# A fused decoder layer: the mLSTM's value products move 65 columns instead of 128

## What is computed

```
qk = einsum('bhsd,bhtd->bhst', qh, kh) / sqrt(64)
C  = qk * D                                   # D: causal decay weights from the gates
normalizer = maximum(abs(sum(C, axis=-1)), exp(-max_log_D))
h  = einsum('bhst,bhtd->bhsd', C / (normalizer + EPS), vh)
h  = (h - mean(h)) * rsqrt(var(h) + 1e-5) * outnorm_scale     # per head
```

## Time and profile before

| | |
|---|---|
| median of 3 runs | 722.97 us (722.48 to 723.44) |
| span of the profiled execution, first to last instruction | 720.5 us |
| its own time outside the span | not listed apart; the median of the runs is 2.5 us over the span |
| TensorE (PE) busy | 622.3 us, 86% |
| weight loads (PEld) busy, beside PE | 451.7 us, 63% |
| VectorE (DVE) busy | 602.0 us, 84% |
| ScalarE (ACT) busy | 566.9 us, 79% |
| GpSimd (POOL) busy | 505.9 us, 70% |
| granted TensorE clock, mean | 0.955 of full speed |
| period of one sequence in the middle of the run | 37.6 us |

### The profile page before, as it was taken

One profiled execution on the slowest core, in us unless ns is written; L12 is line 12 of the kernel. 1 busy time (PEld: TensorE's weight loads), 2 busy tenths in 40 slices (PEclk: granted clock), 3 DMA queues, 4 the chain that ended last, 5 costly groups with the idle time before them and its releaser, 6 DMA issues. The chain is left out here.

```text
span 720.5 us, 16641 instructions
## 1 busy us (share of the span) xinstructions
PE 622.3 (86%) x4892; PEld 451.7 (63%) x4892; DVE 602.0 (84%) x2387; ACT 566.9 (79%) x1189; POOL 505.9 (70%) x781
## 2 busy tenths in 40 slices
PE   5688998999999999999999999998988978684642
PEld 3465785777767676867686868676665746452311
DVE  2475798999999999999999999998979998685853
ACT  1165979899998989898989898988769687875531
POOL 3185678778897878888888888875968746644432
PEclk9599999999999999999999999999999999898856
DMA  8995939455556575647273737454194611111201
GB/s 237 142 214 119 131 76 137 98 89 123 85 104 103 104 105 101 106 93 114 78 113 83 115 66 132 70 100 79 57 131 82 115 42 46 21 61 37 73 16 44
DMA packets 106104, 69.20 MB, mean 96 GB/s; under 512 B 47200, under 2 KB 106016, under 8 KB 106016
## 3 DMA queue, kind: packets, MB, share of 16 engines
q1 hardware_dynamic: 106016, 68.14, 51.9%
HBM read 28.73 MB, written 4.26 MB: 46 GB/s over the span
## 5 line engine op out<-in xcount | busy, mean ns | idle before, releaser
L2774 DVE CUSTOM_DVE_ANT_0 sc<-pS,bias 128x256 f32<-128x256 f32 x512 | 198.5, 415 | 25.6 <-PE pS L291 18.4
L1444 POOL TENSOR_SCALAR sc<-sc,mx 128x256 f32<-128x256 f32 x336 | 166.5, 506 | 28.1 <-DVE mx L2774 27.0
L1895 ACT ACTIVATE pr<-pT 128x512 f32<-128x512 f32 x256 | 152.2, 614 | 16.4 <-PE pT L309 16.1
L309 PE MATMUL pT<-ident,sc 128*128 128x128 f32 x1024 | 152.9, 276 | 6.8 <-POOL sc L1444 3.8
L309 PEld LDWEIGHTS pT<-ident,sc 128*128 128x128 f32 x1024 | 118.0, 141 | 29.7 <-issue 14.7
L291 PE MATMUL pS<-ks,qs 96*128 96x256 bf16 x512 | 94.0, 275 | 7.8 <-DVE mx L2774 6.8
L1883 ACT ACTIVATE sc<-sc,mx 128x256 f32<-128x256 f32 x176 | 90.8, 528 | 3.5 <-DVE mx L2774 3.5
L291 PEld LDWEIGHTS pS<-ks,qs 96*128 96x128 bf16 x512 | 44.2, 98 | 42.6 <-DVE mx L2774 23.0
L326 PE MATMUL pO<-pr,va 128*32 128x256 f32 x1024 | 68.7, 386 | 0.6 <-ACT oT L1905 0.6
L1411 POOL TENSOR_TENSOR rs<-ve,minus_half 128x2 f32<-128x2 f32 x48 | 37.6, 782 | 33.1 <-DVE ve L2805 33.0
L1466 POOL TENSOR_SCALAR hq<-h 128x512 bf16<-128x512 f32 x64 | 38.5, 618 | 29.0 <-ACT h L2094 27.7
(11 more groups left out here) (291 smaller groups left out, 1672.9 us busy)
## 6 DMA issues: line engine op xcount, KB each, us to landing
qs<-parts SPq DMA_DIRECT2D x96, 128.0 KB, 4.7
ks<-parts SPq DMA_DIRECT2D x96, 128.0 KB, 4.9
mb<-mrows SPq DMA_DIRECT2D x16, 512.0 KB, 3.8
xin<-in_x SPq DMA_DIRECT2D x16, 256.0 KB, 3.6
xb<-in_x SPq DMA_DIRECT2D x16, 256.0 KB, 5.3
cx<-in_ctx SPq DMA_DIRECT2D x32, 128.0 KB, 2.1
out<-hq SPq DMA_DIRECT2D x16, 256.0 KB, 2.2
bias<-in_L_attn_pos_bias SPq DMA_DIRECT2D x4, 768.0 KB, 9.2
```

The costliest lines, as they stand in the source:

```text
L309: ins = pe.transpose(bank[:, kt * S + t * P:kt * S + t * P + P], sc[:, s % RING, t, kt * P:kt * P + P], ident[:])
L1444: ins = pool.tensor_scalar(sc[:, s % RING, t, :], sc[:, s % RING, t, :], -1.0, mx[:, s % RING, t:t + 1], ALU.mult, ALU.add)
L1895: act.activation(flat(pr[:, s % RING, :, :]), pT[s % 2][:, :], ACT.Exp, scale=-1.0)\
L2774: dve.tensor_tensor_reduce(out=sc[:, s % RING, t, :], in0=pS[s % 2][:, t * S:t * S + S], in1=bias[:, s, t * P:t * P + S][:, ::-1], scale=1 ...
```

## The change

The context buffer becomes [128, 2, 2, 130]: for each half of the columns (a pair of heads) one column of ones, 128 context columns, one column of ones. An even head reads columns 0 to 64 (ones, then its values), an odd head columns 65 to 129 (its values, then ones); both are one contiguous piece of 65. The three matmuls of a head move 65 columns. The stationary operands, the number of instructions and their order on each engine stay the same, but for one memset that POOL gets at the start. `load_ctx` writes each row in two pieces of 512 bytes instead of one of 1 KB; its first call waits for the memsets. `cv` has 66 columns per head, so that the values always stand in columns 1 to 64 and the sum stands in column 0 or 65.

```
-        cx = sb("cx", [P, TT, D + XD])
+        cx = sb("cx", [P, TT, KT, P + 2])
+        ones = sb("ones", [P, XD])
-        cv = sb("cv", [P, TT, XH, XD + 1])
+        cv = sb("cv", [P, TT, XH, XD + 2])
-        ones = cx[:, 0, D:D + XD]
+        XW = XD + 1
-        G_ALL, G_IDENT, G_GATES = 13, 4, 6
+        G_ALL, G_IDENT, G_GATES = 14, 4, 6
@@ mem_values (TensorE)
-                def vo(t):
-
-                    v = cx[:, t, hh * XD:hh * XD + XD]
-                    return bass.AP(tensor=v.tensor, offset=v.offset, ap=[list(v.ap[0]), [D - hh * XD, 2], [1, XD]])
-
-                pe.matmul(bank[:, 0:P], m[:, 0:P], vo(0), start=True, stop=True)
-                pe.matmul(bank[:, P:S], m[:, P:S], vo(0), start=True, stop=False)
-                pe.matmul(bank[:, P:S], m[:, S:S + P], vo(1), start=False, stop=True)\
+                a, i = hh // 2, XW * (hh % 2)
+                pe.matmul(bank[:, 0:XW], m[:, 0:P], cx[:, 0, a, i:i + XW], start=True, stop=True)
+                pe.matmul(bank[:, P:P + XW], m[:, P:S], cx[:, 0, a, i:i + XW], start=True, stop=False)
+                pe.matmul(bank[:, P:P + XW], m[:, S:S + P], cx[:, 1, a, i:i + XW], start=False, stop=True)\
                     .then_inc(cv_ps.sem, 1)
@@ ctx_turned (TensorE)
-                transposes(bank, cx[:, :, 0:D], ident[:], cxT_ps)
+                for kt in range(KT):
+                    for t in range(TT):
+                        ins = pe.transpose(bank[:, kt * S + t * P:kt * S + t * P + P],
+                                           cx[:, t, kt, 1:P + 1], ident[:])
+                ins.then_inc(cxT_ps.sem, 1)
@@ load_ctx (SP)
+                    if c == 0:
+                        sp.wait_ge(g_set.sem, G_ALL)
-                        sp.dma_start(cx[:, t, 0:D], ctx[c][t * P:t * P + P, :])\
+                        sp.dma_start(cx[:, t, :, 1:P + 1], ctx[c][t * P:t * P + P, :].rearrange("p (a d) -> p a d", a=KT))\
@@ POOL, once
             step(pool.memset(cx[:], 1.0))
             step(pool.memset(am[:], 0.0))
+            step(pool.memset(ones[:], 1.0))
@@ mem_out (ACT)
-                act.activation(cv[:, :, hh, :], bank_of(f"cv{hh}", c)[:, 0:S].rearrange("p (t d) -> p t d", t=TT)
-                               [:, :, 0:XD + 1], ACT.Copy).then_inc(cv_sb.sem, 1)
+                act.activation(cv[:, :, hh, hh % 2:hh % 2 + XW], bank_of(f"cv{hh}", c)[:, 0:S].rearrange("p (t d) -> p t d", t=TT)
+                               [:, :, 0:XW], ACT.Copy).then_inc(cv_sb.sem, 1)
@@ head_stats, head_moments, head_centred (DVE)
-                    dve.bn_stats(hst[:, t, hh, :], cv[:, t, hh, 0:XD]).then_inc(gn_v.sem, 1)
+                    dve.bn_stats(hst[:, t, hh, :], cv[:, t, hh, 1:XW]).then_inc(gn_v.sem, 1)
-                total = cv[:, :, :, XD]
+                total = cv[:, :, :, :].rearrange("p t (a i) d -> p t a (i d)", i=2)[:, :, :, 0::2 * XW + 1]
-                                         cv[:, :, :, :].rearrange("p t h d -> p (t h) d")[:, :, 0:XD], ALU.mult,
+                                         cv[:, :, :, :].rearrange("p t h d -> p (t h) d")[:, :, 1:XW], ALU.mult,
```

More of the change, by code:

```diff
@@ L266, in weight_mean @@
                 for half in range(2):
-                    ins = pe.matmul(bank[64 * half:64 * half + 64, 0:1], ones, w_abs[:, i:i + 1],
+                    ins = pe.matmul(bank[64 * half:64 * half + 64, 0:1], ones[:], w_abs[:, i:i + 1],
                                     start=True, stop=True)
@@ L2836, in head_moments @@
                 dve.tensor_tensor(hmv[:, 2, :, :], half(2, 0), half(2, 1), ALU.add).then_inc(gn_v.sem, 1)
-                dve.scalar_tensor_tensor(nrm[:, 0, :, :], total, -1.0, total, ALU.mult, ALU.max).then_inc(gn_v.sem, 1)
+                dve.scalar_tensor_tensor(nrm[:, 0, :, :].rearrange("p t (a i) -> p t a i", i=2), total, -1.0, total,
+                                         ALU.mult, ALU.max).then_inc(gn_v.sem, 1)
             def head_spread(f):
```

## The result

The changed kernel takes 727.7 us in the median of 13 runs (723.91 to 729.45), the kernel before on the same chip 722.48 (13 runs, 720.47 to 726.89). The ratio is 1.0062, 95% interval 1.0045 to 1.0079: **slower by 0.6%**, where 720.9 us and a range from 718.8 to 724.3 were forecast.

What follows compares the result with a forecast made beforehand. PE's queue was taken to bound the middle, with DVE next; in the closing part only waited-for products count. 720.5 less 2.1 gives a span of 718.4 us, plus 2.5 for the median 720.9 us, range 718.8 to 724.3.

Steps and rivals of the forecast that it cites:

- The bound: Middle periods: PE's queue, busy 98%, bounds, so a nanosecond saved is nearly one of time; DVE 2.0 us per period behind.
- The moved columns, within a product: Six passes of a value product: weight loads keep the spacing near 0.11 us; 0.005 us saved per product.
- The rival by which all passes go to 0.06 us: Value products: moved columns set the spacing, 19 us less of PE's queue; 711 us, 704 at most; chance 0.07.
- The end of a product: After a product's last pass, next work starts sooner: 0.155 us per sequence; with inner spacings 0.175, together 2.1 us showing.
- The late next that I named: Middle periods: PE's wait for POOL's `sc` (L1444), 0.27 us per period, may grow; 0.2 us let be lost in waits.
- The load of the context: 512-byte pieces at `load_ctx`: landing 2.3 us instead of 2.1, covered by 1.4 us of slack before PE turns the context.
- context lands too late: At `ctx_turned`: PE waits 0.3 us in each sequence, up to 1 us once; 726.4 us; chance 0.11.
- The closing part: Last five sequences: of 0.9 us saved by shorter products 0.4 counted, since PE has idle time there.
- Odd column starts: Products starting at column 65 and transposes at column 1: any slowing hides behind the weight loads.
- the memset: POOL's memset of 64 columns at the start, where POOL then idles 10.31 us: costs nothing.
- the wait on SP: SP's first wait for POOL's memsets: no cost, since the first context is fetched long after.
- ACT and DVE: ACT's copy and DVE's reads keep their sizes, stride from 65 to 66 elements: cost 0.

Runs made afterwards that it cites:

- e7: Changed kernel with two context buffers and the loads of sequences 12 and 13 issued earlier; 722.96 us, 1.0013 against the kernel before.
- e9: Changed kernel with two buffers and early loads, 65 moved columns in sequences 0 to 10, 128 in 11 to 15; 723.47 us, 1.0006 against before.
- e1_load: Kernel before with only the new buffer and load in two pieces per row, still 128 moved columns; 726.63 us, 1.0043 against before.
- e3_double: Changed kernel with two context buffers, a load waiting for the products of the last sequence but one; 723.42 us, 1.0014 against before.
- e0_after: The changed kernel run again without an edit; 727.57 us, 1.0066 against the kernel before.
- e2_prod: Kernel before with its old load, products moving 65 adjoining columns, sum left out for three of four heads; 722.31 us, 0.9997 against before.
- e11: Changed kernel with two buffers and early loads, 128 moved columns in sequences 0 to 10, 65 in 11 to 15; 723.29 us, 1.0020 against before.
- e10_wide: Changed kernel with two buffers and early loads, but 128 moved columns in all sequences; 724.1 us, 1.0026 against before.
- e8_before_double: Kernel before with two context buffers and the loads of sequences 12 and 13 issued earlier; 722.49 us, 1.0002 against before.
- e6: Kernel before with its old load, 16 moved columns per pass, 48 of 64 values and the sums left out; 724.6 us, 1.0038 against before.

## Where the prediction went wrong

*The bound.* Right in the main. The middle follows PE's queue, though not one to one: 0.16 us are gone from the four products, 0.07 to 0.11 from the period.

*The moved columns, within a product.* Right, and now shown rather than argued: weight loads stay at 192 ns, two passes at 0.22 us with 65 and with 16 columns. One sign of being right didn't come: a MATMUL's own duration was to fall by some 0.05 us and stayed at 275 ns with 65 columns. The rival by which all passes go to 0.06 us is out.
*The end of a product.* The size was right in PE's queue, and partly by luck, for the places were others. I had 0, 0.05, 0.05 and 0.055 us at the ends of the four products and 0.02 within them; measured are 0.05, 0.01, 0.05 and 0.05. In the starts of the matmuls nothing is gained from the last pass to the next work (250.38 to 250.61 us for two passes of L442, 0.23 as before, so not the 0.06 that I named for the last); it stands between a product's first and second pass. Behind head 1 the change to 64-row products costs as much after the shorter pass. What reaches the period is too large in my sum: of 1.9 us in the middle I let 0.2 be lost, and an undisturbed period shows 0.07 to 0.11, so 0.8 to 1.2 us over eleven sequences instead of 1.7. (The last two products of sequence 10 start at 475.8 and 479.2 us, behind the 474 us that I gave; this changes little.) From sequence 1 to sequence 9, e7 and e9 need 300.1 us where before needs 300.7. The late next that I named, POOL's `sc`, takes 1.1 us in four waits in 202.6 to 428.6 us, less than in the earlier trace rows, so it isn't shown as the taker.

*The load of the context.* **This is the step that failed**: "I take 2.3, nearer the row with the same size and the same queue. That is covered." The median landing was 2.7 us; that the issue would grow I had left out altogether, and it went from 0.43 to 0.61 us for each of two loads in a row. Together they move the second half's landing from 2.5 us after the first issue to 3.4, while PE wants it at 3.9. I then compared a median with a slack. The row that I had before me said 2.0/2.1/4.2, and the loads near 4.2 are those that decide: with a fetch of instructions on the same DMA engines a context lands 4.0 to 5.5 us after the first issue instead of 3.3 to 3.7, and five of the seven late ones were now a wait of 0.3 to 1.5 us. I had written one such case into the range, with 0.2 us. In the runs it cost about 3 us alone (e1_load), and 4 came back once SP needn't wait (e3_double against e0_after).

*The rival "context lands too late"* named the place (`ctx_turned`), the sign and nearly the size (726.4 for 727.7 us), by another path: not a landing of 3.8 us each time, but 2.7 us and a few of over 4. That the size fits is in part luck: the rival had 5.5 us of waits less a gain of 2.1, while the profile has 2.3 us more of waits and a smaller gain. Its chance of 0.11 was too small, and since the range left it out, so was the range.

*The closing part.* I let the shorter products save 0.4 us there. No saving shows: e2_prod, without any change in the load, loses 2.2 us there in its profile (466 us to the end take 256.7 us, against 254.5), more than it gained in the middle, and its time is level. Of these 2.2 us, 1.6 are the fall of the clock at 501 us, which isn't set by the width. I read the clock of 0.91 as given and did not ask what moves it.

*Odd column starts, the memset, the wait on SP, ACT and DVE.* Nothing of them shows in the traces: with odd starts a product takes no longer, and the busy times of ACT and DVE differ by under 1 us. No run tests them one by one.

**What stays open.** Removing every wait for the context leaves the new form level with the old one, though the products' gain of 0.5 to 1 us is in the middle. That a lower clock in the closing part takes it is supported by the clocks above, by the 1.6 us that one fall costs, and by last products at half speed in the profiles of after, e0, e7 and e11 (34.5 to 35.4 us from sequence 14 to 15, where the ten others have 32.7 to 32.9). That the moved columns are what lowers the clock there is a correlation over one profile per kernel and isn't shown: no run moves the clock alone. Also e10_wide (the new load, no waits for it, before's columns) stands at 1.0026 and e8_before_double (the old load) at 1.0002, with intervals that overlap: a further price of the new load, in other transfers of the same queue, is possible and not shown. And half of the medians' difference lies in executions of which there is no profile. No version beat the kernel before.

## What to carry to other kernels

Before a moving operand is narrowed, look at what the passes behind it load: with 128 float32 weights each, the load sets the spacing, and only one distance per product gets shorter. A change of layout that cuts a DMA's rows has its price at the issuing queue as well as at the landing; add both, and set them against the slack of the *worst* sequence, not of the median one. If such a load must stay, give it a second buffer or split it by the part that is free first, which here won back 3 to 4 us. And look at the last products of an execution: a fall of the clock that begins before them cost 1.6 to 2.6 us here, about as much as was to be gained.

## What the runs showed of the hardware

- Within a product, a float32 pass with 128 stationary columns follows the last after 0.11 us with 128, 65 and 16 moved columns alike. Only the second pass of a product that comes after other work follows its first sooner: after 0.11, 0.06 and 0.03 us (before, after, e6).
- Issue time on SP doesn't go with the number of pieces alone. One DMA of 128 KB took a median of 432 ns to issue with 128 pieces of 1 KB, 608 with 256 of 512 bytes, 626 with 512 of 256 bytes, and 378 with 256 of 512 bytes when it was cut by columns over both row tiles. Landing medians were 2.1, 2.7, 2.7 and 2.4 us. The Trainium skill (DMA: Bandwidth & Descriptors, Specifications) puts the smallest transfer for line rate at 512 bytes. Both loads satisfy that rule, and yet the new one landed 0.6 us later; whether the rate or a cost per piece makes this, no run shows. The time of the issue counts for more: the old load with two buffers, issued earlier (e8_before_double), has a landing median of 4.4 us.
- Fetches of instructions (q8 and q14, 41 of 16 KB and some 50 of 8 KB in an execution) run on the same 16 DMA engines as the data: one of 16 KB lies ahead of nearly every late landing, in the kernel before as well, where such a landing comes 4.0 to 4.7 us after the first issue instead of 2.5 to 3.1.
- The granted clock of the partly idle closing part was 0.90 or 0.91 in all six profiles with 128 moved columns and 0.87 to 0.89 in all eight with 65 or 16, although as many matmuls ran. That the width is the cause isn't shown.
- A fall to 1.2 GHz for 3.4 us in a stretch where PE is mostly busy cost 1.6 us (44.2 against 42.6 us for the period). It came in five of 14 profiles; in e7 it followed the same waits of PE, of 0.8 and 1.0 us, that e9 has without a fall.
